# A fused two-layer transformer kernel: hidden rows of both networks turned by DMA from 16-bit halves in SBUF, and one key pair moved a unit later

## What is computed

```
x = x + cross_self_attention(layernorm(x), ctx)   # 16 heads of 128, 4 key/value heads, keys = ctx + own tokens
x = x + down0(silu(gate0(h)) * up0(h))            # h = layernorm(x); "first network"
        # gate0, up0, down0: Hadamard rotation of the row, 8-bit rounding by the row's largest
        # value, product with ternary weights; hidden width 1024
x = x + linear_attention(layernorm(x), ctx)       # feature map, key-value sums, sigmoid gate, output product
x = x + experts(layernorm(x))                     # "second network": 8 experts of hidden width 128, softmax router,
        # top 2 of 8: sum_e p_e * down_e(silu(gate_e(h)) * up_e(h)), p_e = 0 for the six not taken
```

## Time and profile before

| | |
|---|---|
| median of 3 runs | 1284.8 us |
| profiled execution | 1283.05 us |
| its span in the profile | 1281.2 us |
| granted TensorE clock, mean | 0.979 |
| PE busy | 1174.8 us, 92% |
| DVE busy | 1030.4 us, 80% |
| ACT busy | 823.5 us, 64% |
| POOL busy | 805.6 us, 63% |
| main loop | about 150 to 1065 us |
| first expert product on TensorE | 1198.94 us |
| last addition on DVE (az:13) | 1277.46 us |

### The profile page before, as it was taken

The page is one execution under the profiler, slowest core; times in us unless marked ns, Lnnn a source line. Parts: engine busy times, 40 slices in busy tenths (PEclk is TensorE's granted clock), DMA queues, the critical chain, the costliest instruction groups (busy, mean ns, idle before and its releaser), DMA issues.

```text
span 1281.2 us, 30330 instructions
## 1 busy us (share of the span) xinstructions
PE 1174.8 (92%) x11419; PEld 878.0 (69%) x11419; DVE 1030.4 (80%) x1979; ACT 823.5 (64%) x1917; POOL 805.6 (63%) x1010
## 2 busy tenths in 40 slices
PE   4998699999999999999999999999999986678898
PEld 2544377777778777777778777777777765455557
...
GB/s 290 203 95 4 31 141 178 151 150 159 189 170 157 164 157 159 145 180 187 146 170 149 165 151 164 153 147 163 151 166 153 195 181 207 1 1 1 1 1 34
DMA packets 542689, 173.32 MB, mean 135 GB/s; under 512 B 520368, under 2 KB 535232, under 8 KB 542288
## 3 DMA queue, kind: packets, MB, share of 16 engines
...
q0 software_dynamic: 1024, 3.42, 1.1%
...
## 4 chain that ended last, share of the span: by engine, by line
PE 73%; DVE 15%; DMA 3%; POOL 3%; ACT 3%; issue 3%; SPq 0%; POOLq 0%; DVEq 0%; ACTq 0%
PE PS L1254 15%; PE PS L1256 14%; PE PS L1255 14%; PE PS L1401 8%; PE PS L1397 7%; PE PS L1398 7%; DVE mx L1766 5%; DVE pl L1786 3%; DMA pT_l<-pl 2%; PE PS L1350 2%; PE PS L733 1%; PE PS L711 1%; DMA blk<-in_c_blk 1%; PE PS L1359 1%; DVE f_s L1693 1%
## 5 line engine op out<-in xcount | busy, mean ns | idle before, releaser
L1766 DVE TENSOR_REDUCE mx<-PS 128x1 f32<-128x512 f32 (+2 forms) x512 | 296.1, 621 | 112.4 <-PE PS L1256 110.8
L1397 PE MATMUL PS<-v_h,pT_h 128*128 128x129 f16 (+1 forms) x1856 | 224.9, 221 | 4.9 <-DMA pT_h<-ph 4.8
L1398 PE MATMUL PS<-v_l,pT_h 128*128 128x128 f16 (+1 forms) x1856 | 224.8, 220 | 0.0
L2003 POOL CAST ph<-pr_end 128x705 f16<-128x705 f32 (+1 forms) x128 | 111.0, 867 | 171.6 <-ACT pr_end L1557 171.5
L1557 ACT ACTIVATE pr<-PS,nb 128x1024 f32<-128x1024 f32 x128 | 144.3, 1128 | 69.4 <-DVE nb L1774 69.4
L1254 PE MATMUL PS<-kT_h,qT_h 128*128 128x512 f16 (+2 forms) x512 | 181.9, 355 | 7.7 <-ACT pr L1557 7.7
L1397 PEld LDWEIGHTS PS<-v_h,pT_h 128*128 128x128 f16 (+1 forms) x1856 | 182.4, 98 | 8.4 <-DMA pT_h<-ph 5.5
L1398 PEld LDWEIGHTS PS<-v_l,pT_h 128*128 128x128 f16 (+1 forms) x1856 | 182.4, 98 | 2.7
L1255 PE MATMUL PS<-kT_l,qT_h 128*128 128x512 f16 (+2 forms) x512 | 181.0, 353 | 0.0
L1256 PE MATMUL PS<-kT_h,qT_l 128*128 128x512 f16 (+2 forms) x512 | 180.9, 353 | 0.0
L1786 DVE TENSOR_TENSOR pl<-pr,ph 128x1024 f16<-128x1024 f32 x128 | 175.8, 1373 | 0.0
...
## 6 DMA issues: line engine op xcount, KB each, us to landing
...
pT_h<-ph SPq DMA_TRANSPOSE x128, 4.1
pT_l<-pl SPq DMA_TRANSPOSE x128, 3.6
...
```

The costliest lines, as they stand in the source:

```text
L1397: mm(PS[:, OB, 0:DH + 1], pT_h[0:rows, slot, t, :], v_h[0:rows, par, v, :], start=t == 0, stop=False)
L1398: mm(PS[:, OB, 0:DH], pT_h[0:rows, slot, t, :], v_l[0:rows, par, v, :], start=False, stop=False)
L1766: dve.reduce_max(mx[:, c:c + 1], PS[:, c, 0:cols(u % LT, c)], AX_X).then_inc(mx_part, 1)
L2003: pool.tensor_copy(ph[:, slot, HALF:LAST + w], pr_end[:, 0:BANK + w]).then_inc(pool_hi, 1)
```

## The change

Three things change.

1. In the main loop the job ("kq", 1) moves from the end of unit 4 to the start of unit 5. The ring's order stays.
2. The sixteen TensorE steps ht0 and ht1 go. hx now reads the row hh in SBUF and writes its high half as a 16-bit row (`rows_h`); hl subtracts that from the row (`rows_l`), for the first network on DVE, for the second on POOL. The two row buffers lie in the space of the attention's output weights (wo_h, wo_l), two of each per half of the tokens. A new table TAIL_SP has SP issue, for each tile, two transposing DMAs, of the high row into hT_h and of the low row into hT_l. fw and dn1 wait for both (32 on a semaphore), and a row buffer is written again when the tile two before it has been turned.
3. The second butterfly of tiles 0 and 2 moves from POOL to DVE in both halves, and all four tables are written anew: fw stands earlier, both halves' gate and query products of the linear attention stand ahead of la:00, la:1x, tr3:1x and lo:10 ahead of the first expert product, and TensorE ends with up1:13 dn1:10 dn1:11 dn1:12 dn1:03 dn1:13.

TensorE in units 4 and 5 of a group, before: kq1 (kr is the piece of keys; the bank that kq_lo frees is the one of three jobs before) stands ahead of the values' products.

The diff, cut:

```diff
@@ JOBS_AT
-           [("kq", 5), ("piece", 9), ("kq", 4), ("q", 1), ("kq", 1)],
-           [("kq", 2), ("kq", 3)],
+           [("kq", 5), ("piece", 9), ("kq", 4), ("q", 1)],
+           [("kq", 1), ("kq", 2), ("kq", 3)],
...
@@ the tables
-    ht1:11 dn1:02 ht1:12 ht1:13 dn1:03 dn1:10 dn1:11 dn1:12 dn1:13
...
+    up1:02 rt:10 ga1:10 ga1:03 up1:10 up1:03 ga1:11 dn1:00 up1:11 ga1:12 dn1:01 up1:12 ga1:13 dn1:02
+    up1:13 dn1:10 dn1:11 dn1:12 dn1:03 dn1:13
...
-    rs0:00 rs0:01 rs0:10 rs0:11 b1:00 bp:00 b1:01 b1:02 bp:01 bp:02 b1:03 b1:10 bp:03 bp:10 b1:11 b1:12
-    bp:11 bp:12 b1:13 bp:13 rs1:00 rs1:01 rs1:10 rs1:11 rs2:00 rs2:01 rs2:10 rs2:11
+    rs0:00 rs0:01 rs0:10 b1:00 rs0:11 b1:01 bp:01 b1:02 b1:03 bp:03 b1:10 b1:11 bp:11 b1:12 b1:13 bp:13
+    rs1:00 rs1:01 rs1:10 rs1:11 rs2:00 rs2:01 rs2:10 rs2:11 hl1:00 hl1:01 hl1:02 hl1:10 hl1:03 hl1:11
+    hl1:12 hl1:13
+""")
+
+TAIL_SP = stages("""
+    d0:00 d0:01 d0:02 d0:03 d0:10 d0:11 d0:12 d0:13 d1:00 d1:01 d1:02 d1:10 d1:03 d1:11 d1:12 d1:13
 """)
 
@@
+        rows_h, rows_l = ([[w[:, 4 * (2 * hf + k):4 * (2 * hf + k + 1), :].rearrange("p h n -> p (h n)") for k in range(2)]
+                           for hf in range(2)] for w in (wo_h, wo_l))
@@
+        def rows_turned(net, hf, j):
+
+            return (turned_hi, turned_lo)[hf][j % 2], 8 * NG * UNITS + 32 * (2 * net + j // 2 + 1)
@@ TensorE
-            def turn_hidden(hf, j, done):
-                for f in range(8):
-                    last = pe.transpose(PS[:, bank(hf, 2 * (j % 2) + f // 4), (f % 4) * P:(f % 4 + 1) * P],
-                                        hh[hf][:, j, f * P:(f + 1) * P], ident[:, :])
-                last.then_inc(done, 1)
-
-            def turn_rotating(hf, j):
-                pe.wait_ge(tl[second(hf, j)], nth(second(hf, j), hf, j))
+            def rotate_hidden(hf, j):
+                pe.wait_ge(*rows_turned(0, hf, j))
                 if j < 2:
                     pe.wait_ge(tl["hh"], nth("hh", hf, 3))
-                else:
-                    pe.wait_ge(tl["hl0"], nth("hl0", hf, j - 2))
-                turn_hidden(hf, j, tl["ht0"])
-
-            def rotate_hidden(hf, j):
-                pe.wait_ge(tl["hl0"], nth("hl0", hf, j))
-                if j < 2:
-                    pe.wait_ge(tl["hl0"], nth("hl0", hf, j + 2))
                 else:
                     pe.wait_ge(tl["ro"], nth("ro", hf, j - 2))
                 for k in range(FF // D):
@@ -817,26 +813,22 @@
@@
-            def turn_experts(hf, j):
+            def down_second(hf, j):
+                pe.wait_ge(*rows_turned(1, hf, j))
                 if j < 2:
+                    pe.wait_ge(tl["si1"], nth("si1", hf, 3))
+                else:
                     pe.wait_ge(tl["mu"], nth("mu", hf, 3))
-                else:
-                    pe.wait_ge(tl["hl1"], nth("hl1", hf, j - 2))
-                turn_hidden(hf, j, tl["ht1"])
-
-            def down_second(hf, j):
-                pe.wait_ge(tl["hl1"], nth("hl1", hf, j))
-                pe.wait_ge(tl["hl1"], nth("hl1", hf, 2 + j // 2))
                 o = PS[:, bank(hf, j), 0:D]
                 for f in range(NE):
                     last = three(o, (hT_h[hf][:, j, f * P:(f + 1) * P], hT_l[hf][:, j, f * P:(f + 1) * P]),
                                  (ed_h[:, f, :], ed_l[:, f, :]), f == 0, f == NE - 1)
                 last.then_inc(tl["dn1"], 1)
 
@@ ACT
-            def hidden_hi(hf, j, made, done):
-                if made == "ht0" and hf == 1:
-                    act.wait_ge(tl["wd"], nth("wd", 0, 1))
-                act.wait_ge(tl[made], nth(made, hf, j))
-                copy(hT_h[hf][:, j, :], pair_of(hf, j)).then_inc(tl[done], 1)
+            def hidden_hi(hf, j, net):
+                if net:
+                    act.wait_ge(tl["mu"], nth("mu", hf, j))
+                else:
+                    act.wait_ge(tl[second(hf, j)], nth(second(hf, j), hf, j))
+                if net or j >= 2:
+                    act.wait_ge(*rows_turned(net - (j < 2), hf, (j + 2) % 4))
+                copy(rows_h[hf][j % 2], hh[hf][:, j, :]).then_inc(tl[f"hx{net}"], 1)
@@ DVE and POOL
+        def hidden_lo(eng, hf, j, net):
+            eng.wait_ge(tl[f"hx{net}"], nth(f"hx{net}", hf, j))
+            eng.tensor_tensor(rows_l[hf][j % 2], hh[hf][:, j, :], rows_h[hf][j % 2], ALU.subtract).then_inc(tl[f"hl{net}"], 1)
@@ POOL
+                    else:
+                        hidden_lo(pool, hf, i, int(key[2]))
@@ DVE
-            def hidden_lo(hf, j, made, done):
-                dve.wait_ge(tl[made], nth(made, hf, j))
-                dve.tensor_tensor(hT_l[hf][:, j, :], pair_of(hf, j), hT_h[hf][:, j, :], ALU.subtract).then_inc(tl[done], 1)
@@ SP
+            for key, hf, j in TAIL_SP:
+                net = int(key[1])
+                if (net, hf, j) == (0, 1, 0):
+                    sp.wait_ge(tl["wd"], nth("wd", 0, 1))
+                sp.wait_ge(tl[f"hl{net}"], nth(f"hl{net}", hf, j))
+                for t, rows_of in ((hT_h, rows_h), (hT_l, rows_l)):
+                    sp.dma_start_transpose(t[hf][:, j, :].rearrange("p (f n) -> p f n", n=P), rows_of[hf][j % 2])\
+                      .then_inc(rows_turned(net, hf, j)[0], 16)
```

More of the change, by code:

```diff
@@ L94 @@
 TAIL_PE = stages("""
[L95 to L99, removed]
@@ L100 @@
-    tr3:01 lo:00 lo:01 lg:10 lg:11 lq:10 lq:11 tr2:00 tr2:01 rt:00 ga1:00 la:10 la:11 la:12 la:13 up1:00
-    ga1:01 tr3:10 tr3:11 ga1:02 lo:10 lo:11 up1:01 ga1:03 tr2:10 tr2:11 up1:02 rt:10 ga1:10 up1:03
-    up1:10 ga1:11 ht1:00 ht1:01 up1:11 ga1:12 ht1:02 up1:12 ga1:13 ht1:03 up1:13 dn1:00 dn1:01 ht1:10
-    ht1:11 dn1:02 ht1:12 ht1:13 dn1:03 dn1:10 dn1:11 dn1:12 dn1:13
+    tr0:00 tr0:01 rot:00 rot:01 tq:00 tq:01 ga0:00 up0:00 ga0:01 ga0:02 tr0:10 up0:01 ga0:03 rot:10
+    up0:02 tr0:11 rot:11 up0:03 fw:00 tq:10 tq:11 fw:01 ga0:10 up0:10 ga0:11 up0:11 ga0:12 up0:12 ga0:13
@@ L114 @@
+    sg:10 sg:11 ex:10 hi3:00 ex:11 hi3:01 nm2:00 hi2:00 nm2:01 hi2:01 hi3:10 hi3:11 re:00 si1:00 nm2:10
+    si1:01 hi2:10 hx1:00 nm2:11 hx1:01 hi2:11 si1:02 hx1:02 re:10 si1:10 si1:03 hx1:10 hx1:03 si1:11
+    hx1:11 si1:12 hx1:12 si1:13 hx1:13
 """)
 TAIL_DVE = stages("""
-    st0:00 st0:01 lo0:00 lo0:01 qm:00 qq:00 st0:10 wu:00 wd:00 st0:11 hh:00 lo0:10 wd:01 hh:01 lo0:11
-    hh:02 qm:10 hh:03 qq:10 hl0:00 hl0:01 hh:10 hl0:02 hh:11 hh:12 hl0:03 hh:13 mx:00 hl0:10 cl:00 cl:01
-    mx:01 hl0:11 hl0:12 cl:02 cl:03 hl0:13 ad0:00 ad0:01 st1:00 mx:10 ad0:02 ad0:03 st1:01 lo1:00 cl:10
@@ L120 @@
[L120 to L124, removed]
+    st0:00 st0:01 lo0:00 lo0:01 qm:00 qq:00 wu:00 st0:10 wd:00 hh:00 st0:11 wd:01 lo0:10 hh:01 b2:00
@@ new lines @@
+    lo0:11 hh:02 hl0:00 hh:03 qm:10 hl0:01 qq:10 b2:02 mx:00 hh:10 hl0:02 hh:11 hl0:03 hh:12 b2:10 hh:13
+    hl0:10 hl0:11 cl:00 b2:12 cl:01 mx:01 hl0:12 hl0:13 mx:10 ad0:00 ad0:01 cl:02 cl:10 st1:00 cl:11
+    cl:03 mx:11 ad0:02 lo1:00 ad0:03 cl:12 st1:01 cl:13 ad0:10 ad0:11 st1:10 ad0:12 lo1:01 ad0:13 st1:11
+    lo1:10 mn:00 lo1:11 f:00 mn:01 mn:10 f:01 mn:11 z:00 hd:00 hd:01 f:10 lo3:00 f:11 lo3:01 al:00
+    st2:00 al:01 st2:01 z:10 hd:10 hd:11 lo3:10 lo2:00 lo2:01 lo3:11 al:10 rsub:00 st2:10 ch:00 al:11
@@ L834, in down_second @@
                 last.then_inc(tl["dn1"], 1)
-            stage_of = {"rot": rotate, "tq": turn_first, "ga0": gate_first, "up0": up_first, "ht0": turn_rotating,
+            stage_of = {"rot": rotate, "tq": turn_first, "ga0": gate_first, "up0": up_first,
                         "fw": rotate_hidden, "qt": turn_quantised, "dn0": down_first, "lq": linear_q, "lg": linear_gate,
                         "la": linear_attend, "lo": linear_out, "rt": lambda hf, i: router(hf), "ga1": gate_second,
-                        "up1": up_second, "ht1": turn_experts, "dn1": down_second}
+                        "up1": up_second, "dn1": down_second}
             def tail():
@@ L1133, in tail_dve @@
                         "qm": lambda hf, i: quantise(hf, True), "qq": lambda hf, i: quantise(hf, False), "hh": gated,
[L1134 removed]
+                        "b2": second_butterfly, "hl0": lambda hf, j: hidden_lo(dve, hf, j, 0), "mx": largest,
                         "cl": clip, "ad0": add_first, "mn": min_q, "f": feature, "z": lambda hf, i: sums(hf), "hd": attended,
                         "al": add_linear, "rsub": lambda hf, i: router_shift(hf), "ch": lambda hf, i: choose(hf),
[L1137 removed]
+                        "mu": experts, "az": add_second}
             def tail():
```

23 lines of the change are left out of this document (12 added, 11 removed).

## The result

The changed kernel takes 1270.27 us (median of 10 runs, 1268.73 to 1280.87) against 1286.19 us of the kernel before, run beside it (10 runs); the ratio is 0.9891, 95% interval 0.9875 to 0.9908. So 14 us were gained by the ratio, 15.9 by the medians, where 31 were forecast, and the time lies above the range of 1243 to 1268. The profiled execution took 1270.24 us, its span 1268.4 for 1281.2: 12.8 less.

The account below looks back on a forecast made before the run. Bounds: kq1's bank wait in the main loop, latency then TensorE's work in the tail. From 1283.05 us, −10.8 − 9.5 − 11.1 + 0.4 = −31.0 gives 1252.1, with 1.75 about 1254 us; range 1243 to 1268.

Parts of the forecast that it names:

- (a): Main loop: kq1 a unit later removes most of its wait for the ring's bank, −10.8 us, bounds 0 and −13.2.
- So TensorE can come only 0.57 and most of the 0.22 earlier: Main loop, scores of unit 7: 0.72 of kq1's 0.88 us wait is gained in each of 15 groups.
- Rival B: Main loop: the wait moves to unit 7's exponentials through DVE's lag, or to kq2; time 1265 us, chance 0.12.
- (b): First network in the tail: transposes by DMA and the new order end mx:11 9.5 us earlier, bounds 0 and −16.
- with POOL beside it about 26 us: First network: DVE's list after mx:00, up to mx:10 at 1142 us, takes about 26 us beside POOL.
- the walk: First network: following the four tables with trace durations, mx:00 ends about 1114.6, mx:10 at 1142, mx:11 at 1150.3 us.
- Rival A: First network: DMA pairs take 6 to 9 us, so it gains nothing; time 1263 us, chance 0.18.
- (c): Experts' stage: TensorE is busy throughout, so work that leaves it is time, −11.1 us, bounds −7.0 and −11.1.
- Now ahead of the first expert product: Tail: la:1x, tr3:1x and lo:10 move into waits of the linear attention, bringing the experts' stage saving to 11.1 us.
- the other bound (−7.0): Experts' stage: only −7.0 us if the three moved steps lengthen the way to the first expert product equally.
- (d): End of the experts' stage: the last dn1 is about in time, +0.4 us, bounds 0 and +4.4.
- Rival D: Tail: DMA transposes run one after the other, making the kernel slower, 1316 us at T = 10 per pair; chance 0.05.

Follow-up runs that it names:

- relay_late: Changed kernel with ACT's high half of the output weights moved from unit 4 to the end of unit 5: 1263.05 us, ratio 0.9819.
- pool_narrow: Changed kernel with POOL's half 1 butterflies cut to 8 columns, DVE's second ones there reading half 0's rows (output wrong): 1260.69 us, ratio 0.9818.
- high_half_first: Changed kernel with SP issuing the high row's transpose when the copy is done, not the subtraction: 1269.08 us, ratio 0.9867.

## Why the prediction was wrong

It had the direction right, and the size twice too large. The differences from the sum, by the table at the head: the loop 5.9 us, the first network 6.1, the way to the experts 6.6, the start 2.0, less 2.4 that the experts' stage gave beyond the forecast: 18.2 of 31.0. The range took the bounds of one term at a time, and three terms fell short together.

**(a) The ring's wait: the step "So TensorE can come only 0.57 and most of the 0.22 earlier" stopped one unit short.** The scores of unit 7 do start 0.74 us earlier, counted from ACT's first instruction on the piece in unit 4 (650.83 to 655.05 before, 650.76 to 654.24 after). But two turns stood ahead of them before, kq1 and kq2, and one does now, because only a unit's first job stands ahead of its scores. One turn, 0.44 us, was not saved but put behind. What is left is 0.3; the groups show 0.27, the runs 4.1 to 8.1 us in all. Without the new wait TensorE would have come 0.94 (kq1's wait in this group) + 0.44 earlier; it stands 0.69 of that. The rule that ACT's list ahead of the exponentials decides was right and was shown by relay_late. Rival B had this price (the wait moves) but named the wrong places: the wait is not in DVE's lag nor at kq2. DVE did lose its 0.20 of idle time and nothing followed.

**(b) The first network: the term "with POOL beside it about 26 us" was mis-sized.** From mx:00 to mx:10 the walk gave 27.4 us (1114.6 to 1142); it took 31.6 (1113.6 to 1145.2). The list of instructions was right, mx:10 to mx:11 too (8.3 for 8.3), and DVE's list was the path, as said. What was wrong is the price beside POOL: 4.2 of the 6.1 us. The same stretch takes 22.6 us without POOL's butterflies (pool_narrow). So their price was 9.0, and the walk held 4.8 of it, 2.2 of that by accident: I took POOL's 2.45 us for each b2 on DVE, where it is 1.36 alone and 3.5 beside POOL. The rest, 1.9 us, was lost ahead of mx:00. The walk is in the time of the kernel before, whose loop ends at 1076.25; counted from the loop's end it has mx:00 at 38.3 us, and the trace at 40.2. high_half_first, with 39.0, gives 1.25 of that to the transposes' way.

The rule could have been read before. The short instruction of the earlier trace rows at 1098.94 ends at 1100.17, and the instruction that POOL had begun at 1098.89 ends at 1100.15. The clips of the kernel before, beside POOL, show it in full:

```profile
1131.01 3.46 DVE L1040 TENSOR_SCALAR qi<-qf 128x1024 f16<-128x1024 f32 x2
```

Two take 3.46 us there, where two later ones take 1.34. Besides, the rows are b1:10's and bp:10's; bp:03 began at 1116.31. No term of the sum rests on that.

The sentence of the Trainium skill (GPSIMD Engine Reference, Specifications) on DVE instructions with two SBUF inputs agrees with the subtraction and the butterfly, 2.2 for 1.2 and 1.76 for 0.69 us. It covers the clip, which has one input, only by its other condition, the two-port mode, and no run here tells which mode that instruction was in.

Rival A had a small part: pairs land in 4.5 us, not 6 to 9, and the DMAs' way is worth the 1.25 us ahead of mx:00 and 1.4 in high_half_first's runs. With POOL's work gone the stretch from mx:00 to mx:10 lost 9 us though TensorE still waited 9.8 us for DMAs, so they were not what bound that stretch.

**(c) The way to the experts: the step "Now ahead of the first expert product" was counted once, on the side where it saves.** la:1x, tr3:1x and lo:10 take 4.1 us, and I kept the 39.2 us to the first expert product as it was. I gave this as the other bound (−7.0) and should have taken it, since the text itself said "the same steps lie in it", which they don't. It took 45.8. The 2.5 us beyond the 4.1 are work too, for TensorE's idle time did not grow (7.7 us for 7.9). By form, the down products dn0 between mx:11 and the first expert product, before and after:

```profile
L749 PE MATMUL PS<-wd,qiT 128*128 128x256 f16 x32 | 3.7, 273 | 0.0
```

```profile
L745 PE MATMUL PS<-wd,qiT 128*128 128x256 f16 x48 | 5.9, 272 | 0.9 <-ACT qiT L1481 0.9
```

Two dn0 (16 matmuls, 1.7 us) and one tr1 (0.4) that stood ahead of mx:11 stand behind it now, and lo:10 took 1.8 for the 1.3 of the forecast, as half of it ran at the lower clock. With la:1x 1.9 and tr3:1x 0.9 that makes 6.7 of the 6.8 us that TensorE is busy longer. So mx:11 comes 3.4 us earlier partly because steps were put behind it.

**(c), (d) The experts' stage** gave 13.1 for 10.7. The hundred matmuls less are the 11.1 as worked out, of which 4.1 was paid ahead of the stage. The 2.4 beyond the forecast are the 0.4 of the end that didn't come, since TensorE never waits for dn1:13, 0.3 of idle time that went, and 1.7 of clock: the first 10 us ran at 0.83 before and at 1.00 after. In both traces the granted clock is 0.50, the lower level (1.2 GHz), for a spell near the first expert product: before from 1200 to 1203.2 us, inside the stage, and after from 1194.6 to 1197.8, ahead of it. Before that TensorE had idled 3.2 us up to 1198.3 in the one and 1.7 us up to 1193.9 in the other. The stage is 65.38 or 65.39 us, at full clock, in all nine kernels with the new tables, and in the three with the old order the spell begins about 1 us inside it. So the place of the spell goes with the order; what sets it is open, and the forecast had no term for it.

Rival D is refuted: eight tiles take 3.2 us, and two transposes of one row overlap but for the issue. Its sum was wrong besides: +42 against the old end and the −9.5 can't both stand, so T = 10 gives −10.8 + 42 − 11.1 + 20, about +40 and not +31; and the main loop has its two transposes every 7.2 us, not 6.5. The 1309 ns for one 128x128 tile by DMA that the Trainium skill gives (VectorE: DVE Perf Modes, The three transpose paths) can't be added up over a transfer's tiles: the trace has 0.4 us a tile for 8 tiles and less for 15.
